# Last two columns of four layers cut 256 and 404 wide, projections of the attention layer moved into mid-column, rows of scores from a broadcast column

## What is computed

```python
def reference(x, adj, ...):
    h = relu(layernorm(x)); x = x + layer0(h)   # relu(dinv (adj + I) dinv @ h @ W0)
    h = relu(layernorm(x)); x = x + layer1(h)   # dis adj dis @ h @ W1.T + b1
    h = relu(layernorm(x)); x = x + layer2(h)   # relu(d (adj + I) d @ h @ W2)
    h = relu(layernorm(x)); x = x + layer3(h)

    # layer 3, with hs = h @ W_sa
    scores = s_left[:, None] + s_right[None, :]          # s_left = hs @ a[:512], s_right = hs @ a[512:]
    e      = where(adj != 0, exp(-leaky_relu(scores, 0.01)), 0)
    x_a    = (e / (e.sum(1) + 1e-5)) @ hs                # attention
    x_b    = adj @ (h @ W_gcnb) + b_gcnb
    attn_a = sigmoid([adj @ h, h] @ Wa.T + ba); attn_b likewise
    out    = sigmoid(attn_a * x_a + attn_b * x_b)
```

## Time and profile before

| | |
|---|---|
| time, median of three runs | 1857.56 us (1856.84 to 1861.01) |
| the profiled execution: its own time | 1859.72 us |
| its span, first to last instruction | 1857.9 us |
| TensorE: busy, share of the span | 1789.2 us, 96% |
| VectorE: busy, share | 911.4 us, 49% |
| ScalarE: busy, share | 693.5 us, 37% |
| GpSimd: busy, share | 268.6 us, 14% |
| chain that ended last: share of PE | 86% |
| mean granted clock of TensorE | 0.991 |

### The profile page before, as it was taken

The page is one execution under the profiler, slowest core; times in us unless marked ns, Lnnn a source line. Parts: engine busy times, 40 slices in busy tenths (PEclk is TensorE's granted clock), DMA queues, the critical chain, the costliest instruction groups (busy, mean ns, idle before and its releaser), DMA issues.

```text
span 1857.9 us, 23941 instructions
## 1 busy us (share of the span) xinstructions
PE 1789.2 (96%) x9324; PEld 857.0 (46%) x9324; DVE 911.4 (49%) x1857; ACT 693.5 (37%) x1174; POOL 268.6 (14%) x222
## 2 busy tenths in 40 slices
PE   3989999999999998999999999999999998999998
PEld 1434444454444445444444464444444644444445
DVE  5775755476344443500221132624610567778866
ACT  5664434354332432300121122201100466667656
POOL 0000111021000000000000000301200254455441
PEclk9999999999999999999999999999999999999999
DMA  9974643358655754542323345333332433343323
GB/s 394 361 263 123 181 133 118 101 184 301 209 164 169 231 164 108 164 129 76 110 85 93 99 137 181 102 96 109 100 97 53 131 109 87 108 127 106 114 75 101
DMA packets 158850, 268.98 MB, mean 145 GB/s; under 512 B 34184, under 2 KB 55976, under 8 KB 155516
## 3 DMA queue, kind: packets, MB, share of 16 engines
q1 hardware_dynamic: 158736, 267.45, 46.2%
HBM read 208.79 MB, written 58.59 MB: 144 GB/s over the span
## 4 chain that ended last, share of the span: by engine, by line
PE 86%; DVE 5%; DMA 4%; ACT 3%; issue 2%; SPq 0%; POOL 0%; DVEq 0%; ACTq 0%; POOLq 0%
PE ps L865 23%; PE ps L867 23%; PE ps L866 23%; PE ps L817 16%; PE ps L859 1%; DMA RG<-in_adjT 1%; DMA Ad<-RG 1%; DMA T<-in_adj 1%; DVE T L1111 1%; DVE RG L1097 1%; DMA T<-in_w 1%; ACT T L1406 0%; DVE stage L1311 0%; DMA RG<-Ad 0%; ACT RG L1392 0%
## 5 line engine op out<-in xcount | busy, mean ns | idle before, releaser
L865 PE MATMUL ps<-RG,HB 128*128 128x512 f16 (+1 forms) x2368 | 829.1, 356 | 32.3 <-DVE RG L1097 17.6
L866 PE MATMUL ps<-RG,HB 128*128 128x512 f16 (+1 forms) x2368 | 828.8, 355 | 0.0
L867 PE MATMUL ps<-RG,HB 128*128 128x512 f16 (+1 forms) x2368 | 828.5, 355 | 0.0
L865 PEld LDWEIGHTS ps<-RG,HB 128*128 128x128 f16 x2368 | 233.0, 98 | 272.2 <-DVE RG L1097 20.9
L867 PEld LDWEIGHTS ps<-RG,HB 128*128 128x128 f16 x2368 | 233.0, 98 | 234.6 <-issue 4.2
L866 PEld LDWEIGHTS ps<-RG,HB 128*128 128x128 f16 x2368 | 233.0, 98 | 231.1 <-issue 4.0
L817 PE MATMUL ps<-W,OT 128*128 128x512 f16 (+1 forms) x1320 | 294.0, 382 | 2.3 <-DVE OT L1127 2.3
L1127 DVE SCALAR_TENSOR_TENSOR OT<-ps,OT 128x512 f16<-128x512 f32 (+1 forms) x96 | 53.5, 619 | 385.4 <-ACT OT L1440 385.4
L1097 DVE SCALAR_TENSOR_TENSOR RG<-RG,cS 128x512 f16<-128x512 f32 (+1 forms) x174 | 121.8, 713 | 172.7 <-ACT RG L1392 172.4
L817 PEld LDWEIGHTS ps<-W,OT 128*128 128x128 f16 (+1 forms) x1320 | 129.1, 98 | 162.8 <-issue 9.5
L1580 POOL TENSOR_TENSOR T<-T 128x512 f32<-128x512 f32 (+2 forms) x126 | 169.1, 1342 | 191.5 <-DVE T L1111 190.9
(11 more groups left out here) (189 smaller groups left out, 1123.9 us busy)
## 6 DMA issues: line engine op xcount, KB each, us to landing
RG<-in_adjT SPq DMA_DIRECT2D x253, 256.0 KB, 3.0
RG<-Ad SPq DMA_DIRECT2D x190, 256.0 KB, 2.7
Ad<-RG SPq DMA_DIRECT2D x105, 256.0 KB, 3.3
T<-in_adj SPq DMA_DIRECT2D x14, 1354.0 KB, 8.4
T<-in_adjT SPq DMA_DIRECT2D x62, 256.0 KB, 3.7
HBd<-stage SPq DMA_DIRECT2D x24, 512.0 KB, 3.8
HB<-HBd SPq DMA_DIRECT2D x24, 512.0 KB, 6.5
OT<-in_adj SPq DMA_DIRECT2D x7, 1354.0 KB, 9.2
```

The source lines that it names most:

```text
L865: eng.matmul(o, h[0], hi, start=j == 0, stop=False)
L866: eng.matmul(o, h[0], lo, start=False, stop=False)
L867: last = eng.matmul(o, h[1], hi, start=False, stop=False)
```

## The change

It has three parts. In passes 0 to 3 the last two columns hold tiles 16 and 17 (256 wide) and tiles 18 to 21 (404 wide) instead of 16 to 19 (512) and 20, 21 (148); pass 4 keeps the old ones. In pass 4, from column 25 on, the projection of column g-1 stands after step 8 of column g (in column 29 after step 12) instead of behind its last step, and the row sum of column 29 goes to bank 0. The rows of scores are made by PE from `SL` itself, read as a broadcast column, without DVE's `column`; for columns 26 to 29 they stand from step 1 of the column before instead of from step 6 and 7. The planner's `cost` is now in proportion to the width.

```diff
-ROWS = [(0, 4), (4, 4), (8, 4), (12, 4), (16, 4), (20, 2)]
-CHUNKS = [(p, t0, nt) for p in range(5) for t0, nt in ROWS]
+ROWS = [(0, 4), (4, 4), (8, 4), (12, 4), (16, 2), (18, 4)]
+LAST = [(0, 4), (4, 4), (8, 4), (12, 4), (16, 4), (20, 2)]
+CHUNKS = [(p, t0, nt) for p in range(5) for t0, nt in (ROWS if p < 4 else LAST)]
...
-    return 2.6 if width(key[1]) == 512 else 0.76
+    return 2.6 * width(key[1]) / D
...
-        if g % 6 == 0 and g and j == 3:
+        if g % 6 == 0 and g and j == 3 or g > GE and j == (12 if g == G - 1 else 8):
             project(u, g - 1, g)
...
-        if g % 6:
+        if g % 6 and g < GE:
             project(u, g - 1, g)
...
     for g in range(GE, G):
-        first = AT["agg", g - 1, 6]
+        first = AT["agg", g - 1, 6 if g < GE + 2 else 1]
         for i in range(CHUNKS[g][2]):
-            plan(first + i, "column", g, i)
-            plan(first + i + 1, "row", g, i)
+            plan(first + i, "row", g, i)
...
+        def sum_bank(g):
+
+            return 7 - agg_base(g) if g < G - 1 else 0
...
-                    pe.wait_ge(s_col, s("column", g, i))
+                    t = CHUNKS[g][1] + i
+                    pe.wait_ge(s_dots, NT)
...
-                    eng.matmul(ps[b][:, o:o + r], colb[0:r, i % 2, :], identf[0:r, 0, 0:r], start=True,
+                    eng.matmul(ps[b][:, o:o + r], SL[0:r, t:t + 1].to_broadcast([r, P]), identf[0:r, 0, 0:r], start=True,
                                stop=True).then_inc(s_row, 1)
```

More of the change, by code:

```diff
@@ L534, in gnn_kernel @@
             sem("s_ff"), sem("s_wab"))
-        s_dots, s_sr, s_vdot, s_vnorm, s_shift, s_col, s_mask, s_elo = (
-            sem("s_dots"), sem("s_sr"), sem("s_vdot"), sem("s_vnorm"), sem("s_shift"), sem("s_col"), sem("s_mask"),
+        s_dots, s_sr, s_vdot, s_vnorm, s_shift, s_mask, s_elo = (
+            sem("s_dots"), sem("s_sr"), sem("s_vdot"), sem("s_vnorm"), sem("s_shift"), sem("s_mask"),
             sem("s_elo"))
@@ L918, in _ @@
                     g, = of
-                    b = 7 - agg_base(g)
+                    b = sum_bank(g)
                     pe.wait_ge(s_acc, s("mask", g, NT - 1))
@@ L1259, in _ @@
                     g2 = ps[BANK[3, t0]][:, 0:2 * nt].rearrange("p (t n) -> p t n", n=2)
-                    for r, i, k in ((P, 0, 4),) if nt == 4 else ((P, 0, 1), (TR, 1, 1)):
+                    for r, i, k in ((P, 0, nt),) if t0 + nt < NT else ((P, 0, nt - 1), (TR, nt - 1, 1)):
                         last = eng.scalar_tensor_tensor(at[0:r, t0 + i:t0 + i + k, :], g2[0:r, i:i + k, :], Fk[0:r, 1:2],
@@ L1267, in _ @@
                     eng.tensor_scalar(GB[:, c], at[:, c, 1], 0.5, 0.5, ALU.mult, ALU.add).then_inc(s_gate, 1)
-                elif kind == "column":
-                    g, i = of
-                    t, r = CHUNKS[g][1] + i, rows(CHUNKS[g][1] + i)
-                    n = s("column", g, i)
-                    dve.wait_ge(s_dots, NT)
-                    dve.wait_ge(s_row, n - 2)
-                    eng.tensor_copy(colb[0:r, i % 2, :], SL[0:r, t:t + 1].to_broadcast([r, P])).then_inc(s_col, 1)
                 elif kind == "finish":
@@ L1281, in _ @@
                     dve.wait_ge(s_slack, n)
-                    eng.scalar_tensor_tensor(rsum[:, 0:w], erow[:, 0:w], kc[:, 3:4], ps[7 - agg_base(g)][:, 0:w],
+                    eng.scalar_tensor_tensor(rsum[:, 0:w], erow[:, 0:w], kc[:, 3:4], ps[sum_bank(g)][:, 0:w],
                                              ALU.mult, ALU.add).then_inc(s_rsum, 1)
```

## The result

The changed kernel takes 1881.25 us, median of four runs (1879.76 to 1882.47), against 1857.73 us before (1856.84 to 1861.01) on the same chip: a ratio of 1.012, 95% interval 1.0107 to 1.0133. It is slower by 23.5 us. The forecast was 9.3 us slower, 1866.9 us, and its range ended at 1877: the direction was right, the size was not. The profiled execution took 1881.19 us, near its median; its span is 1879.4 us, 21.5 more than before (the profiled execution of before lay 2 us above its median, so the spans differ by less than the medians).

A forecast was written before the change was run, and what follows sets the result against it. TensorE was busy for 96% of the span, so a change could only win back or add idle time. Terms -21.1 - 7.2 + 5.6 + 21.6 + 10.4 made +9.3 us, giving a median of 1866.9 us, range 1859 to 1877.

The forecast's parts named there:

- columns 5, 11, 17 and the clock behind them, column 6: Last columns of passes 0 to 2: idle time, half clock in projections behind, and column 6's wait go; -21.1 us.
- the 256 wide column 4: Pass 0's 256 wide column: ACT and DVE keep up with splits and posts; 0, with 5 us as other end.
- column 25: rows of scores: Wait for DVE's copy and its half clock go, -7.2 us; a new wait for bank 2 with half clock, +5.6.
- ends of columns 25, 26, 27: With the projection gone, PE waits 5.1 us for `finish` at each, plus 2.1 of half clock; +21.6 us.
- from the end of column 28 on: Column 29 and tail: waits for `finish`, late lo halves, z loads behind column 28's stores; +10.4 us (6 to 14).
- The failed step: In the 256 wide columns, ACT and DVE were taken to carry the posts without delaying PE; 0 to 5 us.
- the third rival: DVE late in 256 wide columns or behind mid-column mixes; +14 to +18 us, 1872 to 1876; 14%.
- The fourth rival: Restores still stop the last columns, as images, restore and writes share SP's queue; +22 us, 1880; 8%.
- The rule weighed: 148 wide matmuls: by the skill's issue-gap rule, dropping them would also save an estimated 4.3 us per pass.
- the first rival: Narrow matmuls cost extra through weight loads not hidden, so wider columns gain more; -8 us, 1850; 6%.

The follow-up runs named there:

- e8: The changed kernel with the two z loads of column 29 issued at its step 15, ahead of the stores of column 28; 1880.74 us.
- e2: The changed kernel with the preparation of layer 1's weights and the factors that follow moved from column 4 to column 5; 1866.91 us.
- e6: The kernel before with new widths in passes 0 to 3, layer 1's weights prepared in column 5, rows of scores from `SL` at their old steps; 1829.19 us.
- e1: The changed kernel with GpSimd's maximum over partitions of layer 1's weights replaced by a copy, output not the reference's; 1875.33 us.
- e10: The changed kernel with GpSimd's maximum for layer 1's weights a copy and DVE's maximum over 64 of 2048 values; one run, 1874.38 us.

## Why the prediction was wrong in size

Each term against the stretch of the two traces that shows it (us, after less before):

| term | predicted | measured |
|---|---|---|
| columns 5, 11, 17 and the clock behind them, column 6 | -21.1 | -21.5 |
| the 256 wide column 4 | 0 (to 5) | +14.75 |
| column 25: rows of scores | -1.6 | -2.0 |
| ends of columns 25, 26, 27 | +21.6 | +21.2 |
| from the end of column 28 on | +10.4 | +10.7 |
| columns 0 to 3 (-1.55) and the rest | 0 | -1.6 |
| sum of the spans | +9.3 | +21.5 |

**The failed step** is in the part on widths: "They carried the same posts in 0.77 us steps with PE waiting for nothing until the restore came, so I take 0, with 5 us as the other end." It was argued from the *posts*, which are planned by time (`later`), and from a column that had nothing else to do. What column 4 also had was a stage planned by *step*, the weights of layer 1. I had counted DVE and ACT there and not POOL, though the trace of before shows ACT standing 9.11 us for POOL in that very column. A wait of ACT that costs nothing was no row of mine, because PE didn't wait; the cover of 10.4 us was 1.15 us from being used up. Halving the step halved the cover to 5.2 us, and PE waited 10.78 us, 12.62 in the whole column. Neither 5 us as the bound nor any rival reached 14.75: the third rival names the place, but gives it "up to 5 us" and DVE as the cause, and its 1872 to 1876 stays short of 1881. The fourth rival's 1880 is near in number only: its mechanism, restores that still stop the last columns, is not there, since columns 5, 11 and 17 are never idle.

**What was right.** The 18.1 us of the three narrow columns and the half clock behind two of them came back in full, -21.5 us in the table. The rows of scores lost the wait of 4.67 us and gained one of 3.56 (3.7 predicted) with 1.8 us of clock (1.9): the row and the step behind it take 4.61 us where 2.81 are due. At the three column ends PE stands 5.04 us each time, for DVE's first multiplication as named, with 5.1 predicted:

```profile
1606.41 0.59 PE L871 MATMUL ps<-RG,HB 128*128 128x512 f16 x1 [5.04 <-DVE T L1292]
...
1606.41:1610.95 4.54, 4.54 (x12) 1.72 (x13) 4.54 (x8) 4.05 (x7) 0.00 (x0) 0.56 0.01 2
1680.93:1685.75 4.82, 4.82 (x12) 1.77 (x13) 4.82 (x9) 4.18 (x8) 0.09 (x1) 0.53 0.01 3
1755.73:1760.69 4.96, 4.96 (x12) 1.87 (x13) 4.96 (x9) 4.32 (x8) 0.23 (x1) 0.51 0.00 0
```

The three windows are the step behind each wait: 4.54, 4.82 and 4.96 us where 2.59 are due, at a granted clock of 0.56 to 0.51. That is 1.95 to 2.4 us each; 2.1 was taken. In the end of the program the steps 0 to 12 of column 29 take 14.19 us (14.4 predicted), the wait for `finish` is 3.46 (3.6), and the tail from there 14.1 us (13.7). The loads of z behind the stores (place 3 of the change) cost 2.8 us of that tail, by e8's trace.

Two comparisons of medians fit this without a trace. e2 less e6 is the whole cost of the mid-column placement with its early rows: 1866.91 - 1829.19 = 37.7 us, where 5.6 + 21.6 + 10.4 = 37.6 was the sum. And e2, the changed kernel without the loss in column 4, is 1866.91 us, where the forecast for the whole was 1866.9. That second agreement is luck in part, since the last row of the table (-1.6) and e2's column 4 (+0.8) offset one another.

**The rule weighed.** The widths 256 and 404 take 27.95 / 256 = 0.109 and 43.73 / 256 = 0.171 us a matmul, on the straight line between 148 and 512, weight loads included. The Trainium skill, page "TensorE: Matmul & The Clock Gate", section "Back-to-back issue gap", has weight loads set part of the spacing at 128 columns (about 81 ns); by that rule the first rival would have gained. No run here shows it: 0.064 us at 148 columns is under that figure.

**What stays open.** How the 7.35 us that e1 leaves in column 4 divide among DVE's maximum, the bias additions and the casts of the weights: the waits say 3.3, 0.3 and 2.4 us, the lengths 2.1, 2.0 and 2.5. Most of the difference is the 1.7 us of half clock that e10 alone has of these four; less that, an estimate, the lengths would say 3.8, 0.3 and 2.5. Why a wait of 2.01 us brought half clock in e10 and one of 3.35 us none in e1 is open, as is what POOL does in the pause beside its maximum. The start of column 4 lies between 299.77 us (e8) and 303.88 us (e10) in kernels that are alike up to there, which was not looked into.

## What to carry to other kernels

When a step gets shorter, look up everything that is planned by step numbers in it, and turn "four blocks ahead" into microseconds at the new width; a wait on an engine that PE doesn't see today is cover that is nearly spent. Follow every engine that feeds the step, also the one with 14% of busy time: an in-order queue of a lightly used engine can hold the one small addition that everything needs, and a rare kind of instruction in it can bring a pause many times its own length. And price the cover before moving it: a projection that stood over `finish` at a column's end cost nothing there, and moving it away cost 7.1 us a column (21.2 us for three).

## What the runs showed of the hardware

- GpSimd's record of a maximum over partitions lasts 0.49 or 0.76 us here, and no addition behind it starts for 7.21 and 7.29 us; behind a copy in the same place the addition starts at once. Ahead of a maximum that follows additions there are 6.07 us without work, about 1 us of them after its input was ready. Both pauses begin with a pair of `MODIFY_POOL_CONFIG`. The Trainium skill, page "GPSIMD Engine Reference", section "Engine selection", sends a reduction along partitions to this engine; by these rows one with a single value per partition keeps the additions behind it from the engine for about 8 us.
- DVE's lo half of a 256 wide block takes 0.45 to 0.49 us, and 1.30 and 1.49 us while GpSimd adds two 128x512 tiles.
- Half clock behind a wait of PE: 1.8 us were lost behind one of 3.56 us, 1.95 to 2.4 behind ones of 5.04, and about 1.6 behind one of 10.78, so the price of the clock did not grow with the wait. A wait of 2.01 us (e10) also cost 1.7 us, while one of 3.35 us (e1) cost none.
- A stationary operand read as a broadcast column of one value per partition costs PE what an ordinary one does: a row of scores takes 0.22 us from either.
